# Third and last attention layers of a gated network as one program, with the last layer's norms among the linear layer's last steps and the value products

## The reference

```
x = x + tanh(g_xattn[i]) * attention_i(layernorm(x), ctx)
x = x + tanh(g_ffn[i])   * ffn_i(layernorm(x))
```

```
xq = fake_quant(x, 8 bits, per row);  kq = fake_quant(kernel, 8 bits, per column)
out = fake_quant(xq @ kq + fake_quant(bias, 16 bits), 8 bits, per row)
```

```
queries = rope(norm(x) @ Wq.T);  keys = rope(ctx @ Wk.T);  values = ctx @ Wv.T
out = softmax(mask(queries @ keys.T * scale)) @ values @ Wd.T
```

## Time and profile before

| | us |
|---|---|
| median of 3 runs | 1742.46 (1742.20 to 1744.84) |
| the profiled execution's own time | 1743.67 |
| its span, first to last instruction | 1741.4 |
| TensorE busy, share of the span | 90% |
| VectorE busy | 52% |
| ScalarE busy | 40% |
| GpSimd busy | 36% |

### The profile page before, as it was taken

One profiled execution on the slowest core, in us unless ns is written; L12 is line 12 of the kernel. 1 busy time (PEld: TensorE's weight loads), 2 busy tenths in 40 slices (PEclk: granted clock), 3 DMA queues, 4 the chain that ended last, 5 costly groups with the idle time before them and its releaser, 6 DMA issues. The chain is left out here.

```text
span 1741.4 us, 25591 instructions
## 1 busy us (share of the span) xinstructions
PE 1570.9 (90%) x8786; PEld 1238.4 (71%) x8786; DVE 901.2 (52%) x1781; ACT 701.5 (40%) x2015; POOL 631.3 (36%) x598
## 2 busy tenths in 40 slices
PE   5897979858889999999999997987899999999976
PEld 4565756547668888888888886765677777777762
DVE  4885558867531212222221234856676677667552
ACT  4442154344334444543543445532333333333321
POOL 3543144466323221330332213414544444444210
PEclk9998999978989999999999999987999999999986
DMA  5001010011221010110101011041221221211001
GB/s 200 1 1 49 25 43 13 1 64 61 67 67 49 13 49 1 61 49 2 49 1 49 16 58 55 31 106 58 73 62 61 67 68 50 73 49 49 13 16 49
DMA packets 27885, 81.41 MB, mean 47 GB/s; under 512 B 3248, under 2 KB 11952, under 8 KB 22768
## 3 DMA queue, kind: packets, MB, share of 16 engines
q1 hardware_dynamic: 26896, 79.44, 13.9%
q10 hardware_dynamic: 864, 0.30, 0.1%
HBM read 69.25 MB, written 10.49 MB: 46 GB/s over the span
## 5 line engine op out<-in xcount | busy, mean ns | idle before, releaser
L380 PE MATMUL bank<-hid_high,wq_high 128*128 128x512 f32 (+1 forms) x640 | 257.8, 403 | 6.6 <-issue 6.4
L380 PE MATMUL bank<-hid_high,wq_low 128*128 128x512 f32 (+1 forms) x640 | 240.5, 376 | 0.3 <-issue 0.3
L380 PE MATMUL bank<-hid_low,wq_high 128*128 128x512 f32 (+1 forms) x640 | 238.9, 373 | 0.0
L1163 DVE SCALAR_TENSOR_TENSOR x_stream<-bank,gates,x_stream 128x512 f32<-128x512 f32 x64 | 48.1, 751 | 350.1 <-PE bank L1255 350.1
L979 POOL TENSOR_TENSOR probs<-probs,small 128x512 f32<-128x512 f32 x64 | 67.1, 1048 | 356.9 <-DVE small L1151 356.9
L1530 ACT ACTIVATE probs<-probs,small 128x64 f32<-128x64 f32 x256 | 86.1, 338 | 156.4 <-DVE small L1602 156.4
L380 PEld LDWEIGHTS bank<-hid_high,wq_high 128*128 128x128 f32 x640 | 122.8, 192 | 30.9 <-issue 9.6
L380 PEld LDWEIGHTS bank<-hid_high,wq_low 128*128 128x128 f32 x640 | 122.7, 192 | 23.8 <-issue 0.7
L380 PEld LDWEIGHTS bank<-hid_low,wq_high 128*128 128x128 f32 x640 | 123.2, 193 | 20.5 <-issue 2.9
L1055 ACT ACTIVATE probs<-pair,small 128x128 f32<-128x128 f32 x256 | 90.5, 366 | 82.7 <-DVE small L1145 82.7
L578 POOL TENSOR_TENSOR probs<-probs,small 128x512 f32<-128x512 f32 x64 | 66.7, 1043 | 132.8 <-DVE small L732 132.6
(11 more groups left out here) (279 smaller groups left out, 4029.9 us busy)
## 6 DMA issues: line engine op xcount, KB each, us to landing
raw_q<-in_L_wq SPq DMA_DIRECT2D x18, 1024.0 KB, 4.9
raw_o<-in_L_wo SPq DMA_DIRECT2D x18, 1024.0 KB, 4.9
values<-ctx_values SPq DMA_DIRECT2D x32, 256.0 KB, 3.9
values_t<-ctx_keys SPq DMA_DIRECT2D x8, 512.0 KB, 3.3
raw_c<-in_L_wkv SPq DMA_DIRECT2D x6, 512.0 KB, 3.8
x_stream<-in_x SPq DMA_DIRECT2D x8, 256.0 KB, 9.6
ctx_keys<-raw_o SPq DMA_DIRECT2D x8, 256.0 KB, 2.0
ctx_values<-raw_o SPq DMA_DIRECT2D x16, 128.0 KB, 2.4
```

Source lines behind the costliest of these rows:

```text
L380: last = k.nc.tensor.matmul(out, stationary(a, c), moving(b, c), start=n == 0, stop=n == total - 1)
L1163: nc.vector.scalar_tensor_tensor(xt, k.bank[7][:], gate, xt, ALU.mult, ALU.add).then_inc(k.x_done, 1)
```

## The change

The two attention layers become one block; the functions take the block as an argument, and the end of the linear layer (slots 19 to 24) moves out of `attention_middle` to the head of `attention_last`, where each engine's list is written out anew. All eight tiles' norms are now made there, between the steps of the linear layer: a tile's statistics follow its update, and the pairs' reciprocal deviations follow at once. The order on TensorE is: linear product 5, groups 21 to 23, product 6, groups 24 and 25, product 7, group 26, then norm transposes of tiles 0 to 3, each behind one group (26 to 29), groups 30 and 31, and then query products 0 to 4 with the norm transposes of tiles 4 to 7 between them. The normalised tiles lie in four places, two in `probs` and two in `keys_t`. Unit 3's weights go to `wo`, behind the last projection of layer 2. VectorE rotates the keys between the low parts of tiles 3 and 4, and the queries between those of 5 to 7. SyncE loads the first output weights and values ahead of the stores of groups 24 to 31, and the keys ahead of the last two. The diff, without changes of indentation and cut to its core:

```diff
@@ -391,0 +392,2 @@
+    if unit == 3:
+        return k.wo[part][:, D * c:D * c + D]
@@ -865 +867 @@
-def attention_middle(k):
+def attention_middle(k, block):
...
@@ -926 +927,0 @@
-    with nc.Block() as block:
@@ -995,2 +996,2 @@
-                    if last and s in (12, 16):
-                        context_weights((s - 12) // 4)
+                if last and s == 12:
+                    context_weights(0)
@@ -1005,3 +1006 @@
-            for s in range(SLOTS + LAG_Y, LIN_END):
-                linear_step(s)
-            next_rstd_gpsimd(k, pool)
+        linear.update(pool=linear_step, pool_weights=context_weights)
@@ -1129,8 +1128,2 @@
-            for g in linear_groups(SLOTS + LAG_Y - 1):
-                context_evict(g)
-            for s in range(SLOTS + LAG_Y, LIN_END):
-                linear_early(s)
-                linear_middle(s)
-                linear_late(s)
-                for g in linear_groups(s):
-                    context_evict(g)
+        linear.update(early=linear_early, middle=linear_middle, late=linear_late, evict=context_evict,
+                      act_weights=context_weights)
...
@@ -1188,3 +1181 @@
-            for s in range(SLOTS + LAG_Y, LIN_END):
-                linear_first(s)
-                linear_second(s, updated)
+        linear.update(first=linear_first, second=linear_second, stats=linear_stats)
...
@@ -1329,8 +1320,2 @@
-            pe.wait_ge(k.exp_done, k.at("exp_done", SLOTS * HEADS))
-            for s in range(SLOTS + LAG_Y, LIN_END):
-                if s - 14 < T:
-                    linear(s - 14)
-                if s - 13 < T:
-                    transposes_x(s - 13)
-                for g in linear_groups(s):
-                    context_group(g)
+        linear.update(transposes=transposes_x, product=linear_product, group=context_group)
...
@@ -1348 +1334 @@
-def attention_last(k):
+def attention_last(k, block, linear):
@@ -1366,0 +1353 @@
+    XN = [k.e[:, 0:512], k.e[:, 512:1024], k.kt[:, 1024:1536], k.kt[:, 1536:2048]]
...
@@ -1433,0 +1420,4 @@
+        for g in range(CTX_GROUPS + LIN_SHARED, CTX_GROUPS + 8):
+            ctx_store(k, sp, g)
+        fetch_ahead(k, sp, "L3", "o", k.lo_w, 16)
+        sp.wait_ge(k.o_psum, k.at("o_psum", 0))
@@ -1436 +1426,3 @@
-            sp.wait_ge(k.roundi_done, k.at("roundi_done", 0))
+        for g in range(CTX_GROUPS + 8, 2 * CTX_GROUPS - 2):
+            ctx_store(k, sp, g)
+        sp.wait_ge(k.roundi_done, k.at("roundi_done", T))
@@ -1437,0 +1430,4 @@
+        for g in range(2 * CTX_GROUPS - 2, 2 * CTX_GROUPS):
+            ctx_store(k, sp, g)
+        for g in (2 * CTX_GROUPS - 2, 2 * CTX_GROUPS - 1):
+            sp.wait_ge(k.ctx_stored[g % 2], ctx_stores(g))
@@ -1453,2 +1448,0 @@
-            prep_gpsimd(k, pool)
@@ -1482,0 +1477,7 @@
+        linear["pool_weights"](1)
+        linear["pool"](19)
+        linear["pool"](20)
+        ln_rstd_gpsimd(k, pool, 0, 1)
+        linear["pool"](21)
+        ln_rstd_gpsimd(k, pool, 1, 2)
+        linear["pool"](22)
@@ -1484,0 +1486,2 @@
+        for p in (2, 3):
+            ln_rstd_gpsimd(k, pool, p, p + 1)
@@ -1513 +1516,2 @@
-            next_rstd_gpsimd(k, pool)
+        for p in range(LATE):
+            ln_rstd_gpsimd(k, pool, p, p + 5)
@@ -1545 +1549,3 @@
-            for t in range(T):
+        def norm_high(t):
+            if t == 0:
+                act.wait_ge(k.ctx_psum, CTX_GROUPS + 8)
@@ -1547 +1553,22 @@
-                if t == 2:
+        def evict(*groups):
+            for g in groups:
+                linear["evict"](g)
+        act.wait_ge(k.y_psum, k.at("y_psum", 0))
+        linear["act_weights"](1)
+        linear["early"](19)
+        evict(20)
+        linear["middle"](19)
+        linear["late"](19)
+        evict(21, 22, 23)
+        linear["early"](20)
+        linear["middle"](20)
+        evict(24, 25)
+        linear["early"](21)
+        evict(26)
+        norm_high(0)
+        evict(27)
+        norm_high(1)
+        linear["early"](22)
+        act.wait_ge(k.lin_psum, T)
@@ -1549,0 +1577,9 @@
+        evict(28)
+        norm_high(2)
+        linear["early"](23)
+        evict(29)
+        norm_high(3)
+        evict(30, 31)
+        linear["early"](24)
+        for t in range(4, T):
+            norm_high(t)
@@ -1572,2 +1607,0 @@
-            prep_vector(k, dve)
...
@@ -1627,0 +1662,36 @@
+        def norm(t):
+            if t % 2 == 0:
+                dve.wait_ge(k.rstd_ready, k.at("rstd_ready", t // 2 + 1))
+            if t >= 4:
+                dve.wait_ge(k.xt_psum, k.at("xt_psum", t - 3))
+            nc.vector.tensor_scalar(XN[t % 4], k.x[:, t * D:(t + 1) * D], NORM["mv"][:, 2 * t:2 * t + 1],
+                                    NORM["rstd"][:, t:t + 1], ALU.subtract, ALU.mult).then_inc(k.xn_ready, 1)
+        first, second, linear_stats = linear["first"], linear["second"], linear["stats"]
+        first(19)
+        second(19, None)
+        linear_stats(1)
+        first(20)
+        second(20, None)
+        norm(0)
+        norm(1)
+        linear_stats(2)
+        first(21)
+        second(21, None)
+        linear_stats(3)
+        ln_low_vector(k, dve, 0)
+        first(22)
+        norm(2)
+        second(22, None)
+        norm(3)
+        linear_stats(4)
+        ln_low_vector(k, dve, 1)
+        second(23, None)
+        linear_stats(5)
+        ln_low_vector(k, dve, 2)
+        second(24, None)
+        for t in (6, 7):
+            linear_stats(t)
+        norm(4)
+        norm(5)
+        ln_low_vector(k, dve, 3)
@@ -1630,2 +1700,11 @@
-            for g in range(AHEAD):
-                query(0, g)
+        norm(6)
+        ln_low_vector(k, dve, 4)
+        norm(7)
+        query(0, 0)
+        ln_low_vector(k, dve, 5)
+        query(0, 1)
+        ln_low_vector(k, dve, 6)
+        query(0, 2)
+        ln_low_vector(k, dve, 7)
+        query(0, 3)
+        query(0, 4)
@@ -1708,3 +1787,33 @@
-            for t in range(T):
-                ln_transpose_tensor(k, pe, t, k.xn_ready)
-                if t >= 6:
+        def norm_transposes(t):
+            pe.wait_ge(k.xn_ready, k.at("xn_ready", t + 1))
+            if t >= 2:
+                pe.wait_ge(k.xt_lo, k.at("xt_lo", t - 1))
+            else:
+                pe.wait_ge(k.pt_sbuf, k.at("pt_sbuf", 0))
+            for c in range(C):
+                last = nc.tensor.transpose(k.bank[2 + t % 2][:, c * P:(c + 1) * P], XN[t % 4][:, c * P:(c + 1) * P],
+                                           k.ident[:])
+            last.then_inc(k.xt_psum, 1)
+        def groups(*numbers):
+            for g in numbers:
+                linear["group"](g)
+        linear["product"](5)
+        linear["transposes"](6)
+        pe.wait_ge(k.exp_done, k.at("exp_done", 0))
+        groups(21, 22, 23)
+        linear["product"](6)
+        linear["transposes"](7)
+        groups(24, 25)
+        linear["product"](7)
+        groups(26)
+        norm_transposes(0)
+        groups(27)
+        norm_transposes(1)
+        groups(28)
+        norm_transposes(2)
+        groups(29)
+        norm_transposes(3)
+        groups(30, 31)
+        pe.wait_ge(k.y_scaled, k.at("y_scaled", T))
@@ -1712 +1821,8 @@
-                    queries(0, t - 6, first=True)
+        queries(0, 0, first=True)
+        norm_transposes(4)
+        queries(0, 1, first=True)
+        norm_transposes(5)
+        queries(0, 2)
+        norm_transposes(6)
+        queries(0, 3)
+        norm_transposes(7)
@@ -1714,2 +1830,2 @@
-            for g in range(2, AHEAD):
-                queries(0, g)
+        queries(0, 4)
+        pe.wait_ge(k.ctx_sbuf, 2 * CTX_GROUPS)
...
@@ -2308 +2425 @@
-LIN_END, LIN_SHARED = 25, 5
+LIN_SHARED = 5
@@ -2313,2 +2430 @@
-    g = CTX_GROUPS + (s - 14 if s < 19 else LIN_SHARED + 3 * (s - 19))
-    return range(g, min(g + (1 if s < 19 else 3), 2 * CTX_GROUPS)) if s >= 14 else range(0)
+    return range(CTX_GROUPS + s - 14, CTX_GROUPS + s - 13) if s >= 14 else range(0)
@@ -2345 +2461 @@
-    for g in range(CTX_GROUPS, 2 * CTX_GROUPS):
+    for g in range(CTX_GROUPS, CTX_GROUPS + LIN_SHARED):
@@ -2347,3 +2462,0 @@
-    fetch_ahead(k, sp, "L3", "o", k.lo_w, 16)
-    for g in (2 * CTX_GROUPS - 2, 2 * CTX_GROUPS - 1):
-        sp.wait_ge(k.ctx_stored[g % 2], ctx_stores(g))
...
@@ -2593,2 +2705,2 @@
-        if 0 <= s - 18 < T:
-            next_stats(s - 18)
+        if s == 18:
+            tile_stats_next(0)
...
@@ -2647 +2759 @@
-def linear_counts(k):
+def linear_weight_counts(k):
@@ -2649,2 +2761,6 @@
-              wint_sbuf=C, scales_psum=1, scales_sbuf=1, inv_ready=T, round_done=T, clip_done=T, int_psum=T, int_sbuf=T,
-              y_scaled=T, xi_ready=T, invi_ready=T, roundi_done=T, clipi_done=T, inti_sbuf=T)
+              wint_sbuf=C, scales_psum=1, scales_sbuf=1)
+def linear_tile_counts(k):
+    k.advance(inv_ready=T, round_done=T, clip_done=T, int_psum=T, int_sbuf=T, y_scaled=T, xi_ready=T, invi_ready=T,
+              roundi_done=T, clipi_done=T, inti_sbuf=T)
```

(10 more changed lines are left out.)

1228 lines of the change are left out of this document (615 added, 613 removed).

## The result

| us | before | changed |
|---|---|---|
| median (lowest to highest), 7 runs each | 1742.20 (1737.12 to 1744.84) | 1735.72 (1734.23 to 1738.95) |
| the profiled execution's own time | 1743.67 | 1735.21 |
| its span | 1741.4 | 1733.2 |

The ratio is 0.997, interval 0.9955 to 0.9984: 6.5 us faster, under half of the 14.0 forecast. Timed once more in a later comparison (`changed_again`) it was 0.9965 [0.9951, 0.9978].

What follows compares the result with a forecast made beforehand. TensorE, 90% busy, was taken as the bound, winnable only in its holes. The walk cut product 5 to first scores from 78.7 to 64.7 us, 14.0 less, so the median goes from 1742.46 to 1728.5; 80% range 1723.0 to 1736.0.

Steps and rivals of the forecast that it cites:

- forecast 5.7: Between group 31 and query 0: the border hole stays, at 5.7 us instead of 5.92.
- the walk: Each engine's new list timed up to the first scores, with 0.1 us from engine to engine.
- 0.3 of rounding: At the first scores: 1195.2 with the collision counted was stated as 1195.5.
- as chosen: Short holes of 0.9 and 1.4 us among the queries: clock cost taken as 0, bound 4.8 us.
- Cost 0; without that cover 2 us: Unit 3's casts and subtractions behind slot 18: bias sum of tile 4 is 2 us late, covered by VectorE's later wait.
- One collision counts, 1 us; bounds 0 and 4.4: GpSimd's split of four heads' query weights beside VectorE's norms, among groups 26 to 31: 1 us lost, bounds 0 and 4.4.
- the margin of 0.1: Ahead of tile 3's norm transposes: low part of tile 1 at 1161.6 against 1161.7, called no slack.
- Norms late between the groups: Rival, 18%: two holes of 1 to 2 us and a clock drop give back 5 to 8 us, about 1735.
- bound 3: Stores behind the 2.1 MB of loads may delay the eviction of group 26: cost 0, at most 3 us.
- The 4.41 us: Hole at 1225.04 in the loop's first slots, said to stay; bounds: nothing, or it vanishes.
- signs I had set for being wrong: Lower clock in groups 26 to 31, ScalarE's evictions waiting for DMA, or the following loop slower than before.
- four steps in a row: Group 31 to query 0: eviction, tile 7's whole numbers, update, then statistics, norms and low part, ending at 1173.1.

Runs made afterwards that it cites:

- changed_again: The changed kernel without an edit, timed again in a later comparison: 1737.09 us, ratio 0.9965 to the kernel before.
- experiment 1: `split3_later`: changed kernel with GpSimd's four subtractions for unit 3's weights moved behind slot 19's bias sum; 1734.42 us, 0.9949 to the kernel before.
- experiment 8: `old_with_split3`: kernel before the change plus four GpSimd subtractions of the same size behind slot 18, result thrown away; 1742.58 us, one execution.
- experiment 2: `no_split_q`: changed kernel with the first four heads' query-weight low parts left out except one column per chunk; 1734.57 us, one execution.
- loads_last: Changed kernel with output weights and first values loaded behind all of the stores; 1736.38 us, 0.9957 to the kernel before.
- integers_first: Changed kernel with ScalarE making tile 7's whole numbers ahead of the last two evictions; 1730.70 us, 0.9918 to the kernel before.
- keys_last: Changed kernel with unit 3's subtractions and loads later, whole numbers and query split earlier, second key half behind query 3; 1723.33 us, 0.9886 to the kernel before.

## Why the prediction was half right

- **The direction and the mechanism hold.** Norms between the groups take the border's work off TensorE's path. The two holes at the border, 5.92 and 6.36 us, became one of 5.46 (forecast 5.7), ended as I had said by the low part of tile 3 behind the last tile's chain. Query 0 took 5.1 us, as forecast. From query 0 to the scores it was 21.7 us against a forecast of 22.3, which is no credit to the walk: the walk itself gave 21.0, and the 1.0 of the collision and 0.3 of rounding stood on top of it, though the collision fell ahead of query 0; the holes ahead of queries 2 and 4 were 1.35 and 1.40 (0.9 and 1.4), and the clock behind them was 1.00, as chosen.
- **The step that failed is the price of two overlaps of GpSimd with VectorE.** The forecast gain of 14.0 us came out at 7.1 in the stretch; 5.0 of the missing 6.9 us belong to the two terms that follow, and the walk had no collision in the one and under a third of its cost in the other.
- **"Cost 0; without that cover 2 us" for the weights of unit 3 was wrong**, and it is 2.6 of the missing 6.9 us. I followed the split's end and the bias sum behind it, on GpSimd's own queue, and there the cover did hold. I did not look at what VectorE does at the same time: the updates and scale factors that free product 5's bank. The signs are experiment 1 (moved away: the hole is 1.91), experiment 8 (the same split in the old kernel: 3.69) and the durations 1.53 and 0.87 in both kernels with that hole. The size of a collision stood in the earlier trace rows, 1.59 against 0.50; I had applied it to one step and not to this one.
- **"One collision counts, 1 us; bounds 0 and 4.4" was too small.** It was 3.4 us, well up towards the upper bound: three instructions of one chain meet the split, TensorE waits 2.66 us, and the clock falls behind it. Removing the split (experiment 2) gives that back. Less the 1.0 in the forecast it is 2.4 of the missing time. The Trainium skill's exclusive lock ("SBUF — State Buffer", "SBUF: two separate sides") gave the price of the strict reading, and the trace agrees with it here: the four instructions grew by 0.5 to 1 us each, GpSimd's being 1.4.
- **The remaining 1.9 us are sizes of the walk.** Without the split (experiment 2) product 6 to query 0 is 32.6 us where I had walked 31.2: 0.83 are the hole that is left ahead of tile 3's transposes (the margin of 0.1 was none), and 0.5 that a group with its transposes takes 3.20 us and not the 3.08 (2.72 + 0.36) of the walk, four times. From query 0 to the scores it is 0.7 over the walk's 21.0, 0.45 of it the hole of 1.35 us that was to be 0.9. Less the 0.3 of rounding this is 1.8.
- **"Norms late between the groups", 18%, about 1735, is what happened**, at 1735.72. It named two holes of 1 to 2 us and a drop of the clock; it was one hole there, of 2.66 us, and one ahead of product 5, which it did not name, and the cause I had written for it (ScalarE's fixed order and its waits for stores) was not the cause. The stores were late (3.41 us, bound 3), and `loads_last` shows that this cost nothing. That the number was inside the range is luck: another mechanism put it there than the one written down.
- **Loop, stores, clock between the groups.** The 4.41 us stayed, the loop was no slower, groups 24 to 29 ran at 1.00. Groups 30 and 31 ran at 0.78 behind tile 3's hole, one of the signs I had set for being wrong, and an eviction waited for a DMA, another. The old stores, which I had 2.72 us apart, went out over 21.20 us for eight groups, 3.0 us apart on average.
- **What the walk could have told.** It had the 5.7 us ahead of query 0 as four steps in a row, "none hidden". The first of them, ScalarE's whole numbers of tile 7, was late for its place behind two evictions that nobody needed as soon. `integers_first` shows that the hole was one of order and not of work. All edits together took the stretch from 110.1 to 94.3 us; the work in it was the same but for half of the keys' rotation, which went behind the scores at the price of 0.4 us there.

## What to carry to other kernels

When work is moved on GpSimd, list what VectorE does in the same microseconds, and ask of each such instruction whether TensorE waits behind it; a collision is free in one slot and costs its length, the hole and the clock in the next. When a hand-written order leaves a hole, follow the last waiting engine back, and see whether it waited for data or for the place of an instruction in a list. When one hole is closed, look for the next one a few steps on before the next edit: here 5.46 us ahead of query 0 became 2.7 ahead of query 2, then 2.64 ahead of query 4, and each further edit let through some of what the one before it had not.

## What the runs showed of the hardware

- **Instructions of one column are slowed too.** A scalar_tensor_tensor of 128x1 took 0.16 us, and 0.64 and 0.87 beside GpSimd's subtraction (1.24 in `keys_last`). I had thought of collisions as a matter of large tiles. Not every form is slowed: in the same chains the statistics (0.68), the greatest value (0.67), the reciprocal of one column (0.16) and tensor_scalar of one column (0.15 to 0.20) kept their length, while scalar_tensor_tensor, and tensor_scalar of 512 columns, grew. The Trainium skill ("SBUF — State Buffer", "SBUF: two separate sides") names as VectorE's side of the lock an instruction with two inputs in SBUF or in a two-port mode; the trace agrees for the first, with 0.16 against 0.87, and shows no mode.
- **The clock and the length of a hole.** Behind a hole of 1.90 us at product 5 the granted clock was 0.85 over the 11.24 us that follow, in the kernel before and in `keys_last`, and these are 11.2 us long in all six kernels with such a hole; behind 1.14 us there, and behind 1.35 and 1.40 us ahead of queries 2 and 4, it stayed 1.00. So the last 0.8 us of that hole cost another 1.6 us. Ahead of query 2 it also stayed 1.00 behind 1.77 us (`no_split_q`) and 1.75 us (`split3_later`), and fell to 0.64, 0.57 and 0.60 over the next 4 us behind 2.69, 2.73 and 3.58 us. Behind a hole of 3.7 us ahead of product 5 the way to product 6 took 11.2 to 12.4 us in five executions whose lists are alike there, and 10.9 in `old_with_split3`, so a longer hole did not always cost more clock than one of 1.9.
- **The same hole can cost differently from one execution to the next.** Ahead of the whole stretch, in code that is the same in all kernels, stands a hole of 2.62 or 2.63 us. These are the two kinds, before and after:

```profile
1088.28 0.50 PE L1255 MATMUL bank<-wo_high,out_high 128*128 128x512 f32 x1 [2.63 <-DVE out_low L1156]
1091.14 0.60 PE L2625 MATMUL bank<-ident,queries_t 128*128 128x128 f32 x4
```

```profile
1088.27 0.80 PE L1246 MATMUL bank<-wo_high,out_high 128*128 128x512 f32 x1 [2.63 <-DVE out_low L1149]
1092.61 0.60 PE L2737 MATMUL bank<-ident,queries_t 128*128 128x128 f32 x4
```

The matmul behind it takes 0.50 us, or 0.69 to 0.80, and the transposes above come 2.86 and 4.34 us behind it. From this matmul to product 0 the granted clock was 1.00 in the kernel before and 0.71 in the changed one. Of the thirteen traces read, six are of the first kind, with 3.95 to 3.99 us from this matmul to product 0, and seven of the second, with 5.29 to 5.58 and once 6.85. So 1.3 us and more hang on nothing that an edit changed. The rest of the spread in product 0's start (1092.1 to 1096.6) is there ahead of this hole. That is why single edits were judged by the stretch and not by the median. What decides between the two kinds was not tried.
